# One expert layer for two batches at a time: a mixture-of-experts stage in attention's layout on one Trainium2 core

## What is computed

```
h = h + attention(layernorm(h))          # 4 heads of 16, softmax over 1056 tokens
h = h + ffn(layernorm(h))
# ffn, for every token:
probs = softmax(x @ gate_w + gate_b)     # 8 experts
cw    = the two largest of probs, zero elsewhere
out   = sum over e of cw[e] * (gelu(x @ W1[e] + b1[e]) @ W2[e] + b2[e])   # 64 -> 128 -> 64, all 8 computed
```

## Time and profile before

| | us |
|---|---|
| runs | 1004.88, 995.42, 988.59 |
| median | 995.42 |
| the profiled execution | 989.01 |
| its span, first to last instruction | 987.2 |
| attention up to the barrier between the two parts | 0 to 745.9 |
| FFN | 745.9 to 987.2 |

### The profile page before, as it was taken

One profiled execution on the slowest core, in us unless ns is written; L12 is line 12 of the kernel. 1 busy time (PEld: TensorE's weight loads), 2 busy tenths in 40 slices (PEclk: granted clock), 3 DMA queues, 4 the chain that ended last, 5 costly groups with the idle time before them and its releaser, 6 DMA issues. The chain is left out here.

```text
span 987.2 us, 16297 instructions
## 1 busy us (share of the span) xinstructions
PE 877.0 (89%) x5964; PEld 354.9 (36%) x5964; DVE 566.0 (57%) x1212; ACT 484.4 (49%) x1165; POOL 139.0 (14%) x148
## 2 busy tenths in 40 slices
PE   5665899998999989999999999998866999898996
PEld 5240322432332342342243243332413445354443
DVE  4035665686784577775567778887131554636331
ACT  0020354564664555664445566665433545555552
POOL 0010100011010011010001101010001343434453
PEclk9965599997999999999979999998757899999998
DMA  8329441037532008724002206100007465382731
GB/s 151 59 46 161 77 54 34 1 47 119 99 64 60 2 3 127 134 38 87 1 2 46 34 3 85 38 14 2 1 16 177 88 144 107 88 174 62 154 74 23
DMA packets 56970, 66.53 MB, mean 67 GB/s; under 512 B 24501, under 2 KB 42561, under 8 KB 56897
## 3 DMA queue, kind: packets, MB, share of 16 engines
q1 hardware_dynamic: 56897, 65.56, 36.2%
HBM read 38.82 MB, written 2.57 MB: 42 GB/s over the span
## 5 line engine op out<-in xcount | busy, mean ns | idle before, releaser
L934 DVE TENSOR_REDUCE max_parts<-bank 128x1 f32<-128x512 f32 x512 | 331.2, 684 | 137.2 <-PE bank L1124 134.9
L856 ACT ACTIVATE probs<-bank 128x384 f32<-128x384 f32 (+1 forms) x768 | 311.8, 465 | 195.1 <-PE bank L1087 194.0
L1087 PE MATMUL bank<-q_stack,k_stack 99*128 99x384 bf16 (+1 forms) x768 | 231.1, 330 | 4.2 <-ACT probs L856 3.7
L1124 PE MATMUL bank<-k_stack,q_stack 96*128 96x512 bf16 x512 | 205.7, 405 | 16.8 <-DMA k_stack<-part 12.9
L1065 PE MATMUL bank<-probs,v_tiles 128*32 128x384 f32 (+1 forms) x1536 | 163.7, 501 | 2.4 <-ACT heads_out L841 2.3
L1087 PEld LDWEIGHTS bank<-q_stack,k_stack 99*128 99x128 bf16 x768 | 72.9, 100 | 205.8 <-ACT probs L856 150.7
L1335 ACT ACTIVATE hid<-bank,biases 128x352 f32<-128x352 f32 x192 | 96.0, 552 | 86.0 <-PE bank L1379 86.0
L1354 DVE SCALAR_TENSOR_TENSOR prod<-bank,biases,cwb 128x352 f32<-128x352 f32 x96 | 55.5, 581 | 118.9 <-PE bank L1367 101.9
L1379 PE MATMUL bank<-x,w 128*128 128x352 bf16 (+1 forms) x576 | 105.3, 320 | 6.3 <-DMA x<-part 6.3
L1367 PE MATMUL bank<-hid,w_sb 128*64 128x352 f32 x384 | 78.5, 488 | 8.7 <-DVE prod L1354 5.1
L815 POOL TENSOR_TENSOR part<-qk_rest,part 128x352 bf16<-128x352 f32 x24 | 20.4, 852 | 396.9 <-DVE part L982 396.9
(11 more groups left out here) (151 smaller groups left out, 647.9 us busy)
## 6 DMA issues: line engine op xcount, KB each, us to landing
cwb<-gates_by_expert SPq DMA_DIRECT2D x16, 1056.0 KB, 12.3
x<-in_x SPq DMA_DIRECT2D x64, 256.0 KB, 8.3
q_stack<-part SPq DMA_DIRECT2D x48, 132.0 KB, 4.5
k_stack<-part SPq DMA_DIRECT2D x48, 132.0 KB, 5.1
x<-part SPq DMA_DIRECT2D x32, 132.0 KB, 2.4
h_res<-h_new SPq DMA_DIRECT2D x4, 528.0 KB, 2.9
recip<-recip_rows SPq DMA_DIRECT2D x32, 66.0 KB, 2.6
h_all<-h_res SPq DMA_DIRECT2D x4, 528.0 KB, 6.2
```

The lines of the kernel that those rows point to most:

```text
L856: nc.scalar.activation(probs[:, group % 3, h, 0:n], src, ACT.Exp, scale=SCALE).then_inc(exp_done, 1)
L934: nc.vector.tensor_reduce(max_parts[:, c, H * j + h, i % 2:i % 2 + 1], src[:, :], AX.X, ALU.max)\
L1087: last = nc.tensor.matmul(bank[:, 0:n], ks[par][0:ROWS + 3, h, P * kt:P * kt + P], qs[par][0:ROWS + 3, h, QC[qc]], start=True, stop=True)
L1124: last = nc.tensor.matmul(bank[:, :], queries(h, j), ks[par][0:ROWS, h, HALF * (i % 2):HALF * (i % 2) + HALF], start=True, stop=True)
```

## The change

1. A pair of batches goes through the FFN together, in attention's layout, with float32 x straight from the norm. One step is one expert and one chunk for both batches. First layer: two float32 matmuls, of rows 0 to 63 and of rows 64 to 127, into two banks. Gelu: one instruction of 2 x 352 columns. Second layer: two float32 matmuls, even batch to the lower half of the output's partitions, odd to the upper. Steps per pair: 24, so 96 in all, as before.
2. TensorE's order: the first layers of two steps, then the second layers of the two steps before.
3. The bf16 split of x and W1 is gone: AT_SPLIT, L542, L620, L623, L626 and the L1263 transfers.
4. The gates are [128, 8, 1056] per pair, loaded in three chunks with a semaphore each, first thing in the FFN.
5. GpSimd adds the residual as the first of its eight additions per chunk; still 96 additions.
6. The fold becomes nine transposes of 128 columns per pair, in three steps through one bank (places 4, 9, 12), each copied out by ScalarE; stores are five per pair.
7. The norm steps are finer (NORM: the root takes five steps instead of one); FIRST_NORM goes from units 57 to 92 to units 52 to 88. VectorE runs the norm step ahead of the product and its products two steps late (LAG). The loop is written out.
8. AT_STACK goes from [3, 26] to [3, 12].

```diff
-AT_STACK = [3, 26]
+AT_STACK = [3, 12]
...
-        FIRST_NORM = {57: [("centre", 0)], 59: [("centre", 1)], 61: [("centre", 2)], 64: [("roots", 0)],
-                      67: [("scale", 0)], 69: [("scale", 1)], 71: [("scale", 2)], 74: [("gates", 0)],
...
+        NORM = [("centre", 0), ("centre", 1), ("centre", 2), ("roots", 0), ("newton", 0), ("newton", 1), ("newton", 2),
+                ("parts", 0), ("scale", 0), ("scale", 1), ("scale", 2), ("gates", 0)] \
+            + [("choose", i) for i in range(6)] + [("turn", 0)]
+        FIRST_NORM = dict(zip([52, 54, 56, 59, 60, 61, 62, 63, 66, 68, 70, 73, 75, 77, 79, 81, 83, 85, 88],
+                              [[step] for step in NORM]))
...
+        N_HID, N_PROD, FOLDS, STORES, LAG = 4, 2, 3, 5, 2
+        cwb = [sb(f"cwb{i}", [P, E, L]) for i in range(2)]
+        hid = sb("hid", [P, N_HID, 2, CH])
+        prod = sb("prod", [P, N_PROD, CH])
...
+        for m, step in zip([0, 1, 2, 3, 4, 4, 5, 5, 6, 7, 8, 9, 10, 11, 12, 13, 14, 15, 16], NORM):
+            AT_NORM.setdefault(m, []).append(step)
+        AT_FOLD = [4, 9, 12]
...
+                    for c in range(NCH):
+                        for bp in range(2):
+                            src = cw_dram.rearrange("e (b l) -> b e l", b=B)[2 * p + bp, :, chunk[c]]
+                            sp.dma_start(cwb[p % 2][D * bp:D * bp + D, :, chunk[c]],
+                                         src.unsqueeze(0).broadcast_to([D, E, CH])).then_inc(cw_loaded[p % 2][c], 16)
...
+                def second_layer(n):
+
+                    p, m = divmod(n, PER_PAIR)
+                    pe.wait_ge(gelu_done, n + 1)
+                    at_least(pe, y_read, n - 1)
+                    for bp in range(2):
+                        last = nc.tensor.matmul(banks[4 + n % 2][D * bp:D * bp + D, 0:CH], w2_sb[:, m % E, :],
+                                                hid[:, n % N_HID, bp, :], start=True, stop=True)
+                    last.then_inc(y_full, 1)
...
+                    at_least(pe, gelu_done, n - 1)
+                    for bp in range(2):
+                        rows = slice(D * bp, D * bp + D)
+                        last = nc.tensor.matmul(banks[2 * (n % 2) + bp][:, 0:CH], w1_sb[rows, e, :],
+                                                xn2[p % 2][rows, chunk[c]], start=True, stop=True)
+                    last.then_inc(hid_full, 1)
+
+                def product(p, c, e):
+                    n = PER_PAIR * p + E * c + e
+                    for k in range(2):
+                        if n % 2 == 0:
+                            first_layer(n + k)
+                        elif n > 1:
+                            second_layer(n - 3 + k)
+
+                def fold_step(p, i):
+
+                    at_least(pe, out_read, FOLDS * p + i)
+                    if i == 0:
+                        pe.wait_ge(summed, PER_PAIR * (p + 1))
+                    if i < 2:
+                        for t in range(4):
+                            first = P * (4 * i + t)
+                            last = nc.tensor.transpose(banks[6][:, P * t:P * t + P], acc[p % 2][:, first:first + P], ident)
+                    else:
+                        last = nc.tensor.transpose(banks[6][0:TXT, 0:P], acc[p % 2][:, IMG:L], ident)
+                    last.then_inc(out_full, 1)
```

More of the change, by code:

```diff
@@ L170, in build @@
         root_work = sb("root_work", [P, 2, 2 * KT + 2])
-        qk_part = x_part = [sb(f"part{i}", [P, L], BF16) for i in range(3)]
-        x_rest = sq
+        xn2 = [xn, sb("xn_odd", [P, L])]
         TILES = 2 * KT + 2
@@ L185, in build @@
         cw_tail = sb("cw_tail", [2 * E, TXT])
-        banks = [bank(f"bank{i}") for i in range(8)]
+        psum = ctx.enter_context(nc.psum_tensor("bank", [P, 8, 512], F32))
+        banks = [psum[:, i, :] for i in range(8)]
         score_bank = banks[0:3]
@@ L250, in sb1 @@
             return phase1.enter_context(nc.sbuf_tensor(name, shape, dt))
+        qk_part = [sb1(f"part{i}", [P, L], BF16) for i in range(3)]
         xt = [sb1(f"x{i}", [P, NPATCH + 1, 4, V]) for i in range(2)]
@@ L585, in norm_vector @@
                 first_guess(dve, norm_bank(p, ROOTS), roots2_step, p)
-                for k in range(3):
-                    newton_step(dve, k, roots2_step, p)
+            elif name == "newton":
+                newton_step(dve, i, roots2_step, p)
+            elif name == "parts":
                 split_roots(dve, roots2_step, p).then_inc(norm_read, 1)
@@ L729, in _ @@
                 sp.dma_start(bias_in[0:E, :], b1).then_inc(setup_loaded, 16)
[L730 to L731 removed]
+                for half in range(2):
+                    sp.dma_start(bias_in[E:2 * E, D * half:D * half + D], b2).then_inc(setup_loaded, 16)
                 sp.wait_ge(preset, 1)
@@ new lines, in build, with run_phase2 @@
+        AT_FOLD = [4, 9, 12]
+        def run_phase2(eng, product, norm_step, fold_step, norm_first=False):
+            for p in range(PAIRS):
+                for m in range(PER_PAIR):
+                    c, e = divmod(m, E)
+                    if not norm_first:
+                        product(p, c, e)
+                    if p + 1 < PAIRS:
+                        for name, i in AT_NORM.get(m, []):
+                            norm_step(eng, name, i, p + 1)
+                    if norm_first:
+                        product(p, c, e)
+                    if p > 0 and m in AT_FOLD:
+                        fold_step(p - 1, AT_FOLD.index(m))
@@ new lines, in store @@
+                def store(p):
+                    sp.wait_ge(out_read, FOLDS * (p + 1))
+                    for bp in range(2):
+                        rows = out[2 * p + bp, 0:IMG, :].rearrange("(v t o) c -> o v t c", t=KT, o=2)
+                        for o in range(2):
+                            sp.dma_start(rows[o], outs[p % 2][V * o:V * o + V, :, bp, :]).then_inc(out_stored, 16)
+                    sp.dma_start(out[2 * p:2 * p + 2, IMG:L, :].rearrange("b t c -> t b c"), out_tail[p % 2][:, :, :])\
+                      .then_inc(out_stored, 16)
@@ L1343, in _ @@
                 run_phase2(nc.scalar, product, norm_scalar, evacuate_out)
[L1344 removed]
+                for i in range(FOLDS):
+                    evacuate_out(PAIRS - 1, i)
             @block.vector
             def _(dve):
[L1348 to L1355 removed]
@@ L1391, in fold_batch @@
-                def fold_batch(b, bp, fills):
-                    pe.wait_ge(norm_read, fills)
-                    at_least(pe, out_read, b)
-                    pe.wait_ge(summed, YPB * (b + 1))
-                    for t in range(KT):
-                        nc.tensor.matmul(banks[6][:, D * t:D * t + D], acc[:, bp, P * t:P * t + P], fold,
-                                         start=True, stop=True)
-                    nc.tensor.matmul(banks[7][0:TXT, 0:D], acc[:, bp, IMG:L], fold, start=True, stop=True)\
-                      .then_inc(out_full, 1)
@@ L1407, in constants @@
+                run_phase2(nc.tensor, product, norm_tensor, fold_step)
+                for k in range(2):
+                    second_layer(PER_PAIR * PAIRS - 2 + k)
+                for i in range(FOLDS):
+                    fold_step(PAIRS - 1, i)
 def constants():
```

287 lines of the change are left out of this document (79 added, 208 removed).

## The result

The changed kernel takes 954.45 us (median; 950.68 to 958.59), the kernel before 992.37 (988.59 to 1004.88) in the runs beside it: a ratio of 0.9631, 95% interval 0.9556 to 0.9706. The forecast of 986 was too high by 32 us, inside its range of 940 to 1014. The likeliest case was "within 2%"; it came out 3.7% faster. Ratios here compare only runs within 1.5% of the fastest of their kernel, so they can differ a little from the ratio of the medians.

The account below looks back on a forecast made before the run. TensorE was taken to set the FFN's pace. FFN -36 (-20, -6, -10) and attention +27 (26 + 18 - 13 - 4) gave -9 on 989.0: 980, or 986 on the runs' footing; range 940 to 1014.

Parts of the forecast that it names:

- The likeliest case: Whole kernel: time within 2% of the kernel before, chance 0.53, against 0.32 for faster and 0.15 for slower.
- The step: FFN: a first and a second layer take 1.54 us instead of 1.75, 20 us less over 96 steps.
- The row halves: FFN first layer: two 64-row matmuls on separate row halves run side by side, 0.79 us a pair instead of 1.58.
- the rival of 1062 us: FFN first layer: the two matmuls run one after the other, +40 us in the FFN, 1062 us in all; chance 0.10.
- The fold: FFN: eight folds of 1.93 us become 36 transposes of 0.2, with 2 us given back at the end; net -6 us.
- The start of the FFN: FFN's first pair: no x to transfer and a smaller first gates chunk cut the 12.8 us start cost; -10 us.
- The choice of experts: FFN norm steps: VectorE, held by GpSimd's additions, makes TensorE wait 3 us per choice, as before; no change.
- The rival of 1001 us: FFN: VectorE behind GpSimd's additions sets the pace in the choice, 15 us more, 1001 us; chance 0.12.
- The shift: Attention: twelve stack transfers ahead delay this small transfer, so TensorE waits 4.4 us in each of six slots; +26 us.
- The clock: Attention: half clock behind each of the six waits for the shift costs 3 us each; +18 us (0 to 27).
- What the stacks give back: Attention, odd slots: ScalarE's wait at unit 36, TensorE's 6.5 us behind it and 6.0 of clock go; -13 us.
- Slot 7: Attention: no weight split and a finer, earlier root remove TensorE's 1.48 us wait and others; -4 us (0 to -8).

Follow-up runs that it names:

- Experiment 6: Changed kernel with TensorE's order one step at a time (one first layer, then one second layer) instead of two steps per block; 970.66 us, FFN 198.1 us.
- experiment 7: Changed kernel with both first-layer matmuls on rows 0 to 63, the even batch computed twice and the odd left out; 1023.1 us in a single run.
- experiment 1: Changed kernel with AT_STACK back at [3, 26], all else as changed; 934.28 us, ratio 0.9293, and 934.59 us when run again.
- experiments 3 to 5: Changed kernel with shift transfers on GpSimd's queue: AT_STACK [3, 12] 964.18 us; [3, 26] 967.70 us; [3, 26] with SyncE keeping the shift's wait 924.48 us.
- experiment 8: Changed kernel with pair 0's norm steps back at the old units, the finer steps kept; 958.0 us, ratio 0.9664.

## Why the prediction was right or wrong

**The step (wrong by 17 us).** The step that failed is "I take 0.79 ... Step: 0.79 + 0.75 = 1.54". I took 0.75 from a block of four instructions and 0.79 from one full matmul that stands alone, and carried them over to blocks of eight. Experiment 6 shows that they are right for blocks of four, and the chain that a block of eight costs 1.33 and 1.39, not twice 0.75 and 0.80. The third and fourth matmul (four instructions) add 1.33 - 0.75 = 0.58, or 1.39 - 0.80 = 0.59, so some 0.16 and 0.21 us belong to each block, however long. The change halves the number of blocks, from 192 to 96, and gains 96 x (1.75 - 1.36) = 37 us where I had 20. The earlier trace rows could not show it, since all blocks of second layers there hold four instructions; but the new order was in the diff, and pairing the steps should have been a term of the sum.

The Trainium skill (TensorEngine Tiling (Array Packing), Key Properties) says that a change of the tiling mode drains TensorE. A first layer of 64 rows by 128 columns and a second of 128 by 64 are two modes, so by that rule every block pays a drain and fewer blocks are cheaper. It gives no price; experiment 6 agrees with the direction. Whether the 0.16 and 0.21 us are this drain or the first weight load of a block, no run here tells.

**The row halves (right).** 0.69 a pair side by side, 1.28 on the same rows (experiment 7): the rival of 1062 us had its price right, 96 x (1.28 - 0.69) = 57 us for my 56 (the FFN grew by 71 with what else got longer), and was not this kernel's case. The Trainium skill (TensorE: Matmul & The Clock Gate, Part 3: Packing small matmuls) agrees: two on separate halves ran 1.28 / 0.69 = 1.9 times faster here.

**The fold (right kind, 2 us short).** I had -6. Transposes of 0.2 each were an overestimate: the nine of a pair take 0.59 + 0.59 + 0.21 = 1.39 us, 0.15 each, so 5.6 instead of some 15 in all: -10, and the end gives back about the 2 us that I said, in three fold blocks and two copies behind one another from 940.10 to 943.65.

**The start of the FFN (right).** From the gelu's table load to the second pair's first step are 46.5 us, where a later pair takes 44.56 including 1.39 of fold: an excess of 3.3 against the 12.8 of before, so -9.5 for my -10. The first product waited for its matmul and not for the gates:

```profile
766.24 1.88 PE L1304 MATMUL bank<-xn,w_sb 64*128 64x352 f32 x8 [2.03 <-PEq L684]
...
776.03 0.58 DVE L1273 SCALAR_TENSOR_TENSOR prod<-bank,biases,cwb 128x352 f32<-128x352 f32 x1 [11.20 <-PE bank L1289]
```

**The choice of experts (the rival rightly not taken, the term too high).** The rival of 1001 us did not happen: second layers wait 0.2 us for VectorE. But the sum also took 3 us for each choice, as before, "so nothing changes", and they did not come: in each of the two middle pairs TensorE waited 3.4 us in the kernel before (2.0 ahead of second layers, 1.4 ahead of the transposed gates) and waits 1.6 now (1.0 for the root's parts, 0.6 for a gelu). VectorE's operations are as slow as feared, 0.92 to 0.93 us beside an addition, in the groups from 766 to 949 us:

```profile
L533 DVE TENSOR_TENSOR gate_e<-logits,top 128x144 f32<-128x144 f32 x3 | 2.8, 928 | 0.1
L552 DVE TENSOR_TENSOR hit<-hit,total 128x144 f32<-128x144 f32 x3 | 2.8, 921 | 0.1
```

The products, with one input in PSUM, still take 0.580 us, as the Trainium skill's lock (SBUF — State Buffer, Who interferes with whom) would have it. The terms together, with 2 for the end: -37 - 10 - 9.5 + 2 = -54.5 of the -58.4. For the other 4 the traces show two things that no term had: these shorter waits, 3.6 us over the two middle pairs, and the last piece of each fold before (L1399, 0.23 us, eight times), 1.8. That is 1.5 more than is missing, which I did not assign.

**The shift (right).** 4.4 us in six slots was the forecast; without slot 0's two waits, which experiment 1 has too (2.5 us), it is 29.0 / 6 = 4.8. The clock, 3 us each, is 2.4 to 3.1: the 12 us behind the six waits were granted 0.74 to 0.80. The reason is borne out as well, with one repair: I argued from ring order, and experiments 3 to 5 show that the backlog holds a transfer of another queue just as long. The same section of the Trainium skill (DMA: Bandwidth & Descriptors, Queues, rings and completion order) says that an engine takes turns between queues, by which the small transfer would pass, but also that its completion mark lands only after every earlier write of that engine, across its queues. The times agree with the second; whether the shift's data or its mark came late, the trace doesn't tell.

**What the stacks give back, and the sum over slots 1 to 6 (right in sum, the terms not steady).** 26 + 18 - 13 = +31 was the forecast; the table gives +25.6, and +26.3 for the edit alone. By slots: 7.4 us each for the delay and its clock, so +22 in the even ones and +22 - 13 = +9 in the odd ones. In the kernel before the edit costs 16.6 in the even slots (one of which, slot 4, is 5 us longer than slot 2 before the edit) and 9.7 in the odd ones. In the new kernel it costs 21.4 in the even slots and gives back 5 in the odd ones, since there ScalarE's same three waits stand in slots of 69 to 75 us where the kernel before had 66 to 71. I had read the price of those waits, 13, from one execution of one kernel; in the other it comes out as 27. The waits themselves are the same, and the difference is the clock behind them (experiment 1). Why it fell longer there, no run here tells, and with 7 us between executions of the same slots the 13 and the 27 are rough.

**Slot 7 (right sign, too small).** -4 forecast, -10 measured. TensorE's wait for the root's parts went, 1.48 to 0.20, and of the 10 the earlier units give 3.5 or more (experiment 8). The rest is in what the change took out of the slot and in the clock, 0.81 to 0.88 over it; I did not try the two apart.

In sum: attention came out 7 us under my term, as 4.6 ahead of slot 1 (within what executions differ by), + 25.6 - 10; and the change's gain was missed because one term of the FFN took the price of an instruction for the price of its place in a sequence.

## What to carry to other kernels

Price matmuls by the block in which they stand: where two shapes alternate, see what a second pair of the same shape adds to a block (here 0.59 us against 0.75 to 0.80), and group as many of a shape as the buffers allow. Keep a small transfer that an engine is waiting for ahead of the large ones, since giving it a queue of its own does not get it past them; and when a transfer is moved to another engine, look at what its wait had been holding back. A wait of TensorE can cost more than its length, by the clock behind it: the six waits of 4.2 to 5.5 us cost 2.4 to 3.1 more each, and taking three of 2.1 to 2.5 us out of the odd slots, 6.8 in all, by three numbers gave 19 us here. The same waits can also cost little, as they did in the kernel before, so compare several executions before you put a price on one.

## What the runs showed that I had not expected

- A block of fp32 matmuls of one shape has a fixed cost of 0.16 to 0.21 us, and every further pair of 352 columns on separate halves costs 0.58 to 0.59.
- A 3 KB transfer from GpSimd's queue lands in 1.7 us alone and in up to 10.6 behind twelve transfers of 132 KB that another engine issued.
- The first mark, some 200 us into the kernel, came at 207.2 in one execution and at 211.9 in another of the same kernel, with a granted clock of 0.86 and 0.81 between 100 and 210 us: half clock behind the start-up waits lasts differently long. That is 5 us of the spread between runs; slots 1 to 6 of one and the same work differ by up to 7 more (474.6 to 481.4).
